# Reordered loads and stores, one expert's weights a step, logits one step later, and the second norm on VectorE, in a cross-attention and mixture-of-experts kernel

## The reference

```
x = x + xattn(layernorm(x), ctx, ctx)      # 4 heads of 64: gates ig, fg = [q,k,v] @ gate_kernel + bias
    cs = cumsum(log_sigmoid(fg)); log_D = cs - cs.T + ig.T (lower triangle); D = exp(log_D - rowmax)
    C = (q @ k.T / 8) * D;  h = C / (max(|sum C|, exp(-rowmax)) + 1e-6) @ v;  norm over 64, times scale
x = x + ffn(layernorm(x))                  # 8 experts, top 2 by router logits
    logits = xf @ router_w.T; weights of the two largest, normalised
    out = sum over the two of weight * (gelu(xf @ w1[e]) @ w2[e])      # 256 -> 1024 -> 256
```

## Time and profile before

| | us |
|---|---|
| median of 3 runs | 759.17 (758.35 to 761.41) |
| profiled execution, its own time | 766.17 |
| its span | 764.3 |
| PE busy / DVE / ACT / POOL | 631.3 / 393.1 / 315.4 / 245.1 |
| first PE instruction of the second phase | 347.73 |

### The profile page before, as it was taken

How to read it: one execution, slowest core, us unless ns; L and a number is a source line. 1 busy time by engine, 2 the same in 40 slices (tenths; PEclk the granted TensorE clock), 3 DMA queues, 4 the chain that set the end, 5 groups by cost and what they waited for, 6 DMA issues and landing times.

```text
span 764.3 us, 18354 instructions
## 1 busy us (share of the span) xinstructions
PE 631.3 (83%) x5879; PEld 504.2 (66%) x5879; DVE 393.1 (51%) x1094; ACT 315.4 (41%) x614; POOL 245.1 (32%) x192
## 2 busy tenths in 40 slices
PE   0684968779898994307999999999999999999991
PEld 0554756566877864206877777777777777777780
DVE  1452746667584555503555555555555555555550
ACT  1451562626444322102444444444444444444440
POOL 1101221626466266710222313233133231331322
PEclk9999856565565555557999999999999999999996
DMA  9878438294462122392385493943947639458321
GB/s 316 284 258 322 155 149 302 92 323 157 142 239 94 35 84 84 112 338 84 51 286 137 87 332 48 307 112 56 310 109 212 208 53 320 100 114 306 56 37 21
DMA packets 58964, 130.52 MB, mean 171 GB/s; under 512 B 6384, under 2 KB 38384, under 8 KB 57904
## 3 DMA queue, kind: packets, MB, share of 16 engines
q1 hardware_dynamic: 44384, 110.91, 40.8%
q0 software_dynamic: 13392, 18.10, 13.3%
q10 hardware_dynamic: 1152, 1.07, 0.4%
HBM read 188.49 MB, written 40.13 MB: 299 GB/s over the span
## 4 chain that ended last, share of the span: by engine, by line
PE 67%; DMA 12%; issue 6%; ACT 5%; DVE 4%; SPq 3%; POOL 2%; ACTq 1%; POOLq 0%; DVEq 0%
PE bank L661 15%; PE bank L647 9%; PE bank L649 9%; PE bank L648 8%; PE bank L663 8%; DMA xa<-in_x 7%; PE bank L540 4%; PE bank L565 3%; PE bank L483 3%; PE bank L525 2%; PE bank L510 2%; DMA out<-ct,dst 2%; PE bank L631 2%; POOL rows L1288 1%; DMA xrow<-rows 1%
## 5 line engine op out<-in xcount | busy, mean ns | idle before, releaser
L647 PE MATMUL bank<-dt,wring 128*128 128x128 f16 x1136 | 199.6, 220 | 2.4 <-ACT ct L824 1.2
L649 PE MATMUL bank<-dt,wring 128*128 128x128 f16 x1136 | 199.7, 220 | 0.0
L648 PE MATMUL bank<-dt,wring 128*128 128x128 f16 x1136 | 199.7, 220 | 0.0
L661 PE MATMUL bank<-wring,ct 128*128 128x512 f16 x568 | 192.5, 379 | 0.9 <-DVE ct L1222 0.7
L822 ACT ACTIVATE dt<-bank 128x512 f32<-128x512 f32 x142 | 84.9, 598 | 217.5 <-PE bank L649 211.0
L1222 DVE TENSOR_TENSOR ct<-dt,ct 128x512 f16<-128x512 f32 x142 | 98.4, 693 | 140.8 <-PE bank L663 99.2
L663 PE MATMUL bank<-wring,ct 128*128 128x256 f16 x568 | 154.8, 273 | 0.0
L1324 POOL DMA_INDIRECT out<-ct,dst x48 | 76.0, 1583 | 216.8 <-DMA out<-ct,dst 92.3
L647 PEld LDWEIGHTS bank<-dt,wring 128*128 128x128 f16 x1136 | 111.7, 98 | 27.0 <-issue 14.3
L648 PEld LDWEIGHTS bank<-dt,wring 128*128 128x128 f16 x1136 | 111.8, 98 | 0.9
L649 PEld LDWEIGHTS bank<-dt,wring 128*128 128x128 f16 x1136 | 111.9, 98 | 0.0
(11 more groups left out here) (140 smaller groups left out, 852.3 us busy)
## 6 DMA issues: line engine op xcount, KB each, us to landing
wring<-wsplit SPq DMA_DIRECT2D x284, 512.0 KB
wring<-in_w SPq DMA_DIRECT2D x16, 1024.0 KB, 11.4
xrow<-rows SPq DMA_DIRECT2D x71, 130.0 KB
wsplit<-wring SPq DMA_DIRECT2D x4, 2048.0 KB, 8.4
wsplit<-wcv SPq DMA_DIRECT2D x4, 2048.0 KB, 7.7
xa<-in_x SPq DMA_DIRECT2D x8, 512.0 KB, 10.7
kT<-in_ctx_t SPq DMA_DIRECT2D x8, 512.0 KB, 10.1
ctn<-in_ctx SPq DMA_DIRECT2D x8, 512.0 KB, 10.1
```

The costliest lines, as they stand in the source:

```text
L647: pe.matmul(o, hi, xT[k][:, c, :], start=(c == 0), stop=False)
L648: pe.matmul(o, hi, xT[k][:, CK + c, :], start=False, stop=False)
L649: mm = pe.matmul(o, lo, xT[k][:, c, :], start=False, stop=(c == CK - 1))
L661: pe.matmul(YP[k][:, 0:2 * D], gh[a][:, m4, :], wring[:, k, w:w + 2 * D], start=(a == 0 and m4 == 0), stop=False, skip_group_check=True)
```

## The change

Four edits. `SPLIT` now splits one expert a step, from step -1 to step 6. SP loads keys and context of group k and x of group k+1 ahead of the stores; the store of an expert and the load that follows it stand in the step after its split, and the store of `x1` is of group l in place of m. In the prologue the constants go ahead of the weights, and keys, context and x of the next groups too. PE's `logits` moves from the end of step T to step T+1, between `turn(n,0)` and `scores(t,0)`. `x1_norm` becomes four DVE instructions in place of `x1_shift`; ACT's four and `nm2` go. On DVE `head_norm`, `head_gamma` and `residual` each stand one place earlier against the router's steps.

```diff
-SPLIT = {-2: (0,), -1: (1, 2), 0: (3,), 1: (4,), 2: (5,), 3: (6,), 4: (7,)}
+SPLIT = {e - 1: (e,) for e in range(NE)}
...
             load_k(0)
+            sp.dma_start(gate_b[:, :, :], gate_b_in).then_inc(s_cst, 16)
             load_c(0)
-            sp.dma_start(gate_b[:, :, :], gate_b_in).then_inc(s_cst, 16)
             load_x(1)
-            load_w(0)
             sp.dma_start(cbf[:, :], cb.bitcast(BF16)).then_inc(s_cbf, 16)
             sp.dma_start(gam[:, :], gamma.rearrange("(o d) -> o d", o=1).to_broadcast([P, D])).then_inc(s_cst, 16)
             sp.dma_start(rwT[:, :, :], rw_t).then_inc(s_cst, 16)
+            load_k(1)
+            load_c(1)
+            load_w(0)
+            load_x(2)
             sp.dma_start(pad[:, :], pad_rows).then_inc(s_prep, 16)
             load_w(1)
 
             def step(T, k, n, t, m, l):
-                if k is not None and k > 0:
-                    if k > 1:
-                        load_x(k)
+
+                if k is not None and k > 1:
                     load_k(k)
                     load_c(k)
-                for e in SPLIT.get(T, ()):
+                    if k + 1 < NG:
+                        load_x(k + 1)
+                for e in SPLIT.get(T - 1, ()):
                     store_w(e)
                     if e + 2 < NE:
                         load_w(e + 2)
-                if m is not None:
-                    store_x1(m)
+                if l is not None:
+                    store_x1(l)
...
                 if n is not None:
                     turn(n, 0)
+                if l is not None:
+                    logits(l)
                 if t is not None:
                     scores(t, 0)
...
                     router_turn(m, 1)
-                    logits(m)
...
-            def x1_shift(g):
+            def x1_norm(g):
                 dve.wait_ge(s_rs2, g + 1)
-                after(dve, s_xn2, 2 * g)
-                dve.scalar_tensor_tensor(nm2[:, :], mv2[:, :, 0], -1.0, rs2[:, :], ALU.mult, ALU.mult
-                                         ).then_inc(s_nm2, 1)
+                after(dve, s_sc[g % 2], 16 * (2 * G * (g // 2) + 1))
+                for b in range(G):
+                    ins = dve.tensor_scalar(rowb[g % 2][:, b, 0:D], xa[:, G * g + b, :], mv2[:, b, 0:1],
+                                            rs2[:, b:b + 1], ALU.subtract, ALU.mult)
+                    if b % 2 == 1:
+                        ins.then_inc(s_xn2, 1)
...
                 if_l(slots)
-                if_m(x1_shift)
+                if_m(x1_norm)
                 if n is not None:
                     cummax(n)
```

More of the change, by code:

```diff
@@ L159, in build @@
         rs2 = sb("rs2", [P, G])
-        nm2 = sb("nm2", [P, G])
         rT = sb("rT", [P, G, CK, P])
@@ L280, in build @@
         s_rs2 = sem("x1_rstd")
-        s_nm2 = sem("x1_shift")
         s_xn2 = sem("x1_normed")
@@ L747, in weights_high @@
                                ).then_inc(s_wh2, 1)
[L749 to L756, removed]
             def router_turned(g, h):
@@ L788, in step @@
                     rows_left(n)
-                if m is not None:
-                    x1_norm(m)
                 if t is not None:
@@ L1090, in if_l @@
                         f(l, *a)
+                if_m(head_norm)
                 if_l(router, 0)
-                if_m(head_norm)
+                if_m(head_gamma)
                 if_l(router, 1)
-                if_m(head_gamma)
-                if_l(router, 2)
                 if t is not None:
                     scores(t, 0, 0)
+                if_l(router, 2)
+                if_m(residual)
                 if_l(router, 3)
-                if_m(residual)
                 if_l(router, 4)
@@ L1263, in x1_rstd @@
                 after(pool, s_xn2, 2 * g)
-                after(pool, s_nm2, g)
                 pool.tensor_tensor(rs2[:, :], ve2[:, :], mhalf[:, 0:G], ALU.pow).then_inc(s_rs2, 1)
```

## The result

The changed kernel takes 726.95 us, the median of four runs (717.89 to 731.93), against 758.76 before (four runs, 755.90 to 761.41). The ratio, of the fast runs alone (two of these four, 717.89 and 724.66), is 0.951, interval 0.941 to 0.960: faster by 4 to 6%. By the medians it is 0.958. Forecast were 739 us, range 720 to 751. The time is in the range and the sign is right, but the gain is 32 us where 20 were forecast. Run once more later, eight times beside other runs of the kernel before, it took 732.19 us (721.32 to 734.73), ratio 0.962 (0.957 to 0.966). That is 30 us, and 0.961 by the medians, so the two measurements agree better than their ratios look.

A forecast was written before the change was run, and what follows sets the result against it. PE, busy 137.8 of 160.1 us in steps 2 to 6, and its clock bound the first phase. Terms -8.7 - 13.4 - 3.8 + 1.6 + 4.0 = -20.3 us, from 759.2, gave 739 us, range 720 to 751.

The forecast's parts named there:

- Prologue: Up to the first logd: constants ahead of weights land earlier, rwT near 10.7 us; -8.7 us, bounds -6.6 and -9.
- Waits for x and for the copies: PE's waits vanish: x -10.1 in step 0, -4.4 in step 1, -9.5 in steps 2 and 3; copies before logits -9.8.
- Rival D: Loads: x or constants still come late behind 2 MB transfers filling the queue; only some 3 us gained, 756; chance 0.09.
- `x1_norm`: Four DVE instructions ahead of cummax take 1.4 us; PE waits 1.1 us a step before max_turn, +5.5 in steps 2 to 6.
- Rival C: x1_norm on DVE held by POOL on the shared memory port, four taking 7.3 us; slower, 774 us; chance 0.05.
- Step 0: No wait for x of group 2, -10.1, and dt only 0.2 us late, -3.3; sum -13.4 us.
- The clock in steps 2 to 6: Moved logits cut PE's run before the clock's rise; three short 2.4 GHz stretches remain in place of 27.5 us: +15.4 us.
- rival B: PE's clock rises as before in steps 2 to 6, since PE has no gaps: 723.5 us; chance 0.21, 0.03 of it for 700.
- The price of an us at 2.4 GHz: From gate products, 6.99 us at the low clock and 3.69 at the high: each us at the high level is worth 0.89.
- a wait for `dt` in steps 1 to 6: Sign of being wrong: PE waiting for dt or ct there, where the new splits were expected to cost nothing.
- Tail: From step 7 to the second phase: expert 7's split delays head_norm, ct and second scores by 3 us; +4, bounds 1 and 6.
- From the profile to the median: Whole kernel: median of runs 7.0 us below the profiled 766.17; so 759.2 - 20.3 = 738.9, called 739.

The follow-up runs named there:

- the loads alone: Kernel before with only SP's new load order, prologue and steps; old splits, logits, norm and DVE order kept: 743.72 us, ratio 0.978.
- the logits back: Changed kernel with logits moved back to the step's end, behind router_turn: 735.83 us, ratio 0.966.
- the gap alone: Changed kernel with PE made to wait at the head of a step for the router_turn copies, instruction order kept: 744.13 us, ratio 0.976.
- The version with hardly a gap left: Changed kernel with ACT's split behind the step's dt and x1_norm behind cummax on DVE: 726.95 us, ratio 0.949.

## Why the prediction was right, and where it failed

**Prologue: right.** `rwT` was forecast for 10.7 and landed at 11.74; the first `logd` for 27.2 to 27.5 and came at 28.48. The 0.3 us for `pad` weren't needed: POOL's `vt` starts at 23.23, right behind its input `gsb`. The late us is that of the load. The cross-check is the experiment with the old prologue: its first `logd` is 6.1 us later and its median 11 us higher, with runs that spread over 16.

**Waits for x and for the copies: right.** Both are gone as forecast: 24 us of `at` in the trace of before, 9.8 of the copies. Rival D is refuted; the loads are early enough in every step.

**`x1_norm`: right.** Forecast 1.4 us for the four and a wait of 1.1 a step. All 32 take 385 to 414 ns, 1.38 us for four, and PE waits 1.12, 0.94, 0.93, 0.94 and 0.66 in steps 2 to 6. Step 1, for which 0.6 was forecast, has no such wait. The nearest row, was the right guide. The rule that I weighed against it, "VectorE: DVE Perf Modes" of the Trainium skill, section "The perf-mode tier table", would have made it 0.8 by my estimate; this form, with two per-partition scalars, did not run at that rate here. Rival C is refuted: `msk` again took 1.83 us beside POOL's `vt`, and no `tensor_scalar` was held, beside `rs` or otherwise.

**Step 0: mechanism right, size off by 5.6 us.** The wait for `at` is gone and that for `dt` is 0.40. What I had not counted is the clock there. PE got 6.8 us at 2.4 GHz already in step 0 (34.3 to 41.1), and the gate products took 3.7 us for 7.0; PE's busy time in step 0 fell from 26.98 to 21.21 us for the same work. The repeated profile has the same stretch, from 34.9.

**The clock in steps 2 to 6: the step that failed.** The prediction put it so: `logits` "now cut the run `logd`, transposes, scores, transposes, after which the clock rose", and took three short stretches, 10.2 us, for +15.4. The changed kernel's two profiles show 40.8 and 30.6 us. In steps 2 to 6 three profiles have the same order, and PE's gaps at the head of a step gone: 10.2 us high took 158.9 us, 30.6 took 148.9, 40.8 took 145.8; the runs took 734.7 (740.85 less the 6.1 of the old prologue), 724.75 and 717.89. The medians of 727 and 732 lie between the first two and so, by an estimate from these three, at some 15 to 26 us high. So on the typical run the count was 5 to 16 us too low, and on the two profiled ones 20 to 31.

What the runs showed in place of that step: the logits, narrow as they are, did not cut the run (they stand within a stretch), and PE's standing still at the head of a step, which the change removed, goes with where the clock rises. Four kernels have a wait of 1.7 to 2.5 us there: before, the loads alone, the logits back, and the gap alone. In steps 2 to 6 of their profiles the first stretch of a step begins 11.3 to 14.2 us after the end of `router_turn`, 17 times out of 18. In the ten profiles without that wait it begins from 0.3 us ahead of this end to 2.2 us behind it, 39 times out of 40. The late rise comes with the logits at the step's end and, in the gap alone, with the logits behind the transposes; the early one comes with them there and behind the second `logd`. So it goes with the gap and not with the place of the logits, though no run has the old place without the gap. I had the reading as rival B and gave it 0.21.

How much of the gain this is stays less clear. With the wait the profiles have 10 to 27 us high, without it 10 to 41, and only the four runs with the gap of 2.4 us lie apart by their mean clock. With the logits back, and the gap 1.7 us as after steps 1 to 3 of before, the medians show no cost beyond the wait. That the gap of the old order cost clock time is therefore not shown.

**The price of an us at 2.4 GHz: right once, too high above that.** I took 0.89 from the gate products. At 10.2 us high the sum made with it holds. But the next 20.4 us were worth 0.49 each, and the 10.2 after them 0.30. Part of this is that a faster PE runs into waits that a slow one does not see: twice 0.97 for `dt` and 4.5 in all before the gates, none of which the profile at 10.2 shows. In the stretch of 10.2 us at 106.0 it was busy for 7.75. The other part is PE's own work: its busy time fell by 14.7 us over those 20.4 (151.13 to 136.45) and by 4.3 over the 10.2 (to 132.15), 0.72 and 0.42 an us, not 0.89. I had called a wait for `dt` in steps 1 to 6 a sign of being wrong; it is there, but small, and only where the clock is up.

**Tail: sized too high.** +4 forecast, +0.9 measured. The second scores of step 7 do wait for `ct`, 2.66 us:

```profile
236.08 2.08 PE L527 MATMUL bank<-qT,kT 64*128 64x128 f32 x16 [2.66 <-DVE ct L898]
```

Step 7 is 1.6 us longer (25.2 against 23.6) and step 8 0.7. The stretch from there to the second phase is 1.4 us shorter.

**From the profile to the median.** I carried the sum over by the 7.0 us between profile and median of before. The changed kernel's runs lie 14 us apart, those of before 5.5, since what a step gets of the high clock differs from one execution to the next: the step that ends in the first profile at 223.0 got 6.8 us at 2.4 GHz and took 28.9, and in the second it got none and took 33.2. On the medians the miss is 12 us (739 against 727), or 7 by the eight later runs. Step 0 (5.6) and the tail (3.1) less the prologue (1.0) make 7.7 of it; what is left for steps 2 to 6, the clock above all, is 0 to 4. In the profiles it looks like 16. The first median lies nearer to rival B's 723.5 than to the 739, the second halfway between them: the range held both readings, so that the time fell in it says little for the count of the clock.

**What stays open:** what decides whether a given step gets one stretch, two, or none in the same kernel. The version with hardly a gap left had 20.4 us high, the changed kernel with more waits 30.6 and 40.8. No run here separates the kind of products from chance, and the count of 15 to 26 us for a typical run is worked out, not seen. And the 4.5 to 9.6 us before the gates have no releaser in the profile; they weren't traced to one.

## What to carry to other kernels

Where PE is the bound and its clock moves between two levels, forecast the kernel at both: the sum for steps 2 to 6 at the low clock was right to 3 us in the one profile that had it, and above it an us at the high level brought 0.3 to 0.5, not the 0.89 by which the gate products get faster; that `dt` and the gates' inputs were then late is a part of it. Look at where in a step the clock rises, too: with a wait of 2 us there it came some 12 us later. One profile of each kernel can misstate such a gain by half (48 us between these traces, 32 between the medians), so read the clock of both before reading a difference. And test the parts of a change together with what they lean on: the new load order without the new table of splits lost 8 us in one wait.

## What the runs showed of the hardware that I had not expected

- Executions of one kernel on one core differ by 2% (717.89 to 731.93 us), and the profiles put it in the first phase: 303.0, 309.4 and, less the old prologue's 6.1, 321.7 us up to the second, with 40.8, 30.6 and 10.2 us of steps 2 to 6 at 2.4 GHz.
- A stop of PE of 2.4 us in a step of 34, added to the changed kernel, lowered the mean granted clock of all four runs to 0.802 to 0.805; without it twelve runs had 0.816 to 0.842. In its profile two of three stretches of steps 2 to 6 begin some 14 us behind `router_turn`, where those of the changed kernel begin within 1.5.
- Products eight columns wide ran at the high level without ending it: 1.85 us for the sixteen against 3.55 at the low level. With PE busy for 19.16 of 20.50 us behind it the clock stayed at 0.50.
- POOL's indirect scatters (`rows`, L1282) took 0.96 us at the least and 2.89 at 112.32, where DVE's second split instruction (two inputs, 2.29 us from 112.01) ran beside the start; the next, of 2.01, lay beside DVE's two products of the head norm (1.22 us each, from 114.21 and 115.47) and more. Their mean went from 1123 to 1257 ns with the change. It is 1148 with the norm behind the maximum and 1118 with the norm on ACT, which has the same splits: so the new table of splits alone does not raise it.

```profile
112.32 2.89 POOL L1282 DMA_INDIRECT rows<-rowb,slot  x1 [0.19 <-issue]
115.51 2.01 POOL L1282 DMA_INDIRECT rows<-rowb,slot  x1 [0.30 <-issue]
117.83 1.63 POOL L1282 DMA_INDIRECT rows<-rowb,slot  x1 [0.30 <-issue]
119.76 0.96 POOL L1282 DMA_INDIRECT rows<-rowb,slot  x1 [0.30 <-issue]
```
